# A graph-transformer network on one core: fp32 recurrent products, the last layer's projections among its graph attention, and norms measured tile by tile

## The chip, the cores and the metric

One Trainium2 chip, one of its cores. The whole network is one program. The metric is the device time of one execution in microseconds (us), the median of three. TensorE (PE) multiplies, VectorE (DVE) and ScalarE (ACT) do elementwise work, GpSimd (POOL) and SyncE (SP) mostly move data.

## The reference

625 nodes, 512 features, four layers on one residual array `X`, each with a graph part, a token mixer and a feed-forward part. Cut to what matters here:

```
L0: three SAGE convolutions (agg@Wl + h@Wr, layer norm, PReLU), linear attention, two small mixtures of experts
L1: two SAGE convolutions, slice attention; then an LSTM over the 625 nodes in order:
    for t in range(625):
        i, f, o, c~ = x[t] @ Wx + h @ Wh + b        # h: 512 values, Wh: 512 x 2048
        c = sigmoid(f) * c + sigmoid(i) * tanh(c~);  h = sigmoid(o) * tanh(c)
L2: linear attention, graph attention with an edge bias (found by sorting the edges), mixture of experts
L3: MLP 512-256-512, then graph attention (GAT):
        alpha[s, d] = exp(leaky_relu(a_src[s] + a_dst[d], 0.2) - max over the edges into d)
    and beside it linear attention on the same normalized X, then a layer norm; gated experts (8 of them)
```

A layer norm without scale, (x - mean) / sqrt(var + eps), stands before each half layer.

## The kernel before

`X` lies as five tiles of 125 rows by 512 columns. Products are in fp32 except those on one-hot and count data and those of the recurrence. Every product goes into one of four PSUM slots in turn (`TILES` gives their order and the engine that empties each); PE waits for a slot's last user. Weights come through a ring of four buffers of 1 MB in the order of `WEIGHTS`, loaded by SP: the load for a buffer waits until the last product of the weight four places earlier has been issued and done. Each engine runs its own program in order; semaphores tie them. `st.after()` on DVE waits for all that DVE itself has counted.

The recurrence (the loop over t). `h` is cut into four chunks of 128 (a column each). Its weights are cut for four strips of TensorE: strip q takes 128 of the 512 columns of each gate and writes PSUM partitions from 32q. The two halves f of the hidden units are worked in turn, so that the elementwise work of one lies beside the other's. In fp32 accuracy this is had from bf16: `Wh` was split before the loop into three bf16 parts (`L1f.split`, DVE, in the ring buffers), and `h` is split every step into three bf16 columns (`hidden_high`, `hidden_mid`, `hidden_low`, the last releasing PE by `ls_h`). `half(f, chunks)` (L929) then issues, for each chunk, part and strip, a product of 3 stationary columns with 256 moving ones: 96 a step. The order of a step:

```
PE:  wait h0; half 0 chunks 0,1; half 1 chunk 0; wait h1; half 0 chunks 2,3 -> full0; half 1 chunks 1,2,3 -> full1
DVE: turn0 (L1796), gather0 (L1801), product0, cell0, turn1, high0 (L1818), gather1, mid0, low0 (L1829), product1, cell1, high1, mid1, low1
ACT: tanh of the gates (L1258), tanh of the cell (L1262) for either half, the next step's x part, `keep` (h to ls_out)
```

`turn` is a 32x32 stream transpose that spreads the strips' results over 128 partitions; `gather` sums them with the x part. In 320 of the 625 steps a step of the edge sort stands between: two bf16 products of PE (L951), one DVE pass, in every second such step two ACT passes.

Norms (`normalize`): five `bn_stats` (L1432), five `bn_aggr` (L1435), a Newton inverse root in 15 small instructions with four rounds (L1414 to L1437), then one pass for each tile (L1447 in `norm_x`). `conv` follows it with scale, shift and PReLU, each as a pass over all five tiles.

The last layer: after `L3.adjT` PE spreads the attention's scalars (`L3.sdB`, L1103), DVE forms ten blocks `pT` of 125x625 in three passes (L2076, L2079, L2083), ACT takes exp, DVE multiplies by the counts (L2086), PE applies them (`L3.gat`), turns the result (`L3.gT`) and multiplies by W3 (`L3.gout`); then come q, k and v of linear attention (`qkv("L3")`), with POOL (`mins`), ACT (`exps`) and DVE (`feature_maps`) for their feature maps, then `attention("L3")`.

## Time and profile before

| | |
|---|---|
| median of three runs | 4932.3 us (4931.12 to 4932.89) |
| the profiled execution's own time | 4929.59 us |
| its span, first to last instruction | 4927.6 us |
| busy in it: PE, DVE, ACT, POOL | 3898.6, 2478.6, 1414.7, 345.7 us |
| mean granted TensorE clock | 0.962 of full speed |

### The profile page before, as it was taken

The page shows a single profiled execution, that of the slowest core. Times are in us where ns is not written, and L with a number is a line of the kernel's source. Part 1 is how long each engine was busy: PE and PEld are TensorE (multiplying, and loading weights), DVE is VectorE, ACT ScalarE, POOL GpSimd, SP SyncE. Part 2 cuts the span into 40 slices and gives each one's busy share as a digit, 9 for nine tenths or more (in the row PEclk, how much of TensorE's full clock was granted, in tenths as well). Part 3 has the DMA queues.
Part 4 walks back from the last instruction along what each step waited for, and adds up shares of the span by engine and source line. Part 5 has one row for each costly group of instructions (what it writes and reads, how often), then busy time and mean ns, then how long its engine had stood idle before and what let it go on. Part 6 is the DMA issues. An engine that isn't in the chain of part 4 may idle for free.

```text
span 4927.6 us, 161288 instructions
## 1 busy us (share of the span) xinstructions
PE 3898.6 (79%) x68148; PEld 2504.9 (51%) x68148; DVE 2478.6 (50%) x10718; ACT 1414.7 (29%) x4675; POOL 345.7 (7%) x314
## 2 busy tenths in 40 slices
PE   9878896877777666777777666666679996789998
PEld 7444453555555444555555444444446744545554
DVE  6323216477767555667776556665542535221111
ACT  0010111344444222444444222245531401011111
POOL 0000000000000222000000221012210000100000
PEclk9888998999999999999999999999999998889999
DMA  2000101200000000000000000000003301011111
GB/s 68 26 30 27 41 26 69 103 27 0 0 0 0 1 1 4 1 0 0 0 0 0 1 2 4 0 1 1 1 24 84 73 30 58 34 37 60 60 60 36
DMA packets 46351, 122.19 MB, mean 25 GB/s; under 512 B 24956, under 2 KB 32915, under 8 KB 35657
## 3 DMA queue, kind: packets, MB, share of 16 engines
q1 hardware_dynamic: 36490, 99.00, 5.9%
q0 software_dynamic: 9776, 22.00, 2.3%
q8 instruction: 60, 0.98, 0.1%
q14 instruction: 25, 0.20, 0.0%
HBM read 105.79 MB, written 14.92 MB: 24 GB/s over the span
## 4 chain that ended last, share of the span: by engine, by line
PE 62%; DVE 28%; issue 5%; ACT 4%; POOL 0%; DVEq 0%; ACTq 0%; POOLq 0%
PE PS L655 31%; PE PS L929 25%; DVE ls_turn L1796 11%; DVE ls_act L1801 4%; ACT ls_gate L1258 3%; PE PS L741 2%; DVE ls_pr L1805 2%; DVE ls_parts L1829 2%; DVE ls_parts L1824 1%; DVE ls_parts L1818 1%; PE PS L1026 1%; PE PS L686 1%; PE PS L1076 1%; DVE stats L1432 1%; PE PS L1016 1%
## 5 line engine op out<-in xcount | busy, mean ns | idle before, releaser
L929 PE MATMUL PS<-BUF,ls_parts 128*3 128x256 bf16 x60000 | 1856.8, 273 | 743.6 <-DVE ls_parts L1829 720.1
L929 PEld LDWEIGHTS PS<-BUF,ls_parts 128*3 128x3 bf16 x60000 | 1318.7, 84 | 1279.7 <-DVE ls_parts L1829 1107.1
L1796 DVE STREAM_TRANSPOSE ls_turn<-PS 128x256 f32<-128x256 f32 x1250 | 557.3, 446 | 488.5 <-PE PS L929 466.2
L655 PE MATMUL PS<-ring,BUF 128*125 128x512 f32 (+1 forms) x1440 | 617.8, 588 | 27.6 <-DVE BUF L1569 11.2
L655 PE MATMUL PS<-BUF,ring 128*128 128x512 f32 (+1 forms) x2176 | 594.6, 435 | 2.3 <-ACT BUF L1166 1.4
L1258 ACT ACTIVATE ls_gate<-ls_act 128x8 f32<-128x8 f32 x1250 | 261.6, 209 | 973.8 <-DVE ls_act L1801 970.5
L655 PEld LDWEIGHTS PS<-BUF,ring 128*128 128x128 f32 x2176 | 330.7, 191 | 273.1 <-issue 271.2
L655 PEld LDWEIGHTS PS<-ring,BUF 128*125 128x125 f32 x1440 | 270.5, 190 | 356.8 <-issue 333.2
L1262 ACT ACTIVATE ls_th<-ls_gate 128x2 f32<-128x2 f32 x1250 | 253.8, 203 | 454.9 <-DVE ls_gate L1810 454.9
L1174 ACT ACTIVATE BUF<-PS,cols 128x625 f32<-128x625 f32 x146 | 114.0, 782 | 712.8 <-PE PS L655 709.9
L1805 DVE SCALAR_TENSOR_TENSOR ls_pr<-ls_gate 128x4 f32<-128x4 f32 x1250 | 203.1, 162 | 178.1 <-ACT ls_gate L1258 173.5
L1818 DVE SCALAR_TENSOR_TENSOR ls_parts<-ls_gate,ls_th 128x2 f32<-128x2 f32 x1250 | 194.0, 155 | 149.9 <-ACT ls_th L1262 132.5
L1801 DVE TENSOR_REDUCE ls_act<-ls_turn 128x8 f32<-128x32 f32 x1250 | 232.3, 186 | 21.5
L1166 ACT ACTIVATE BUF<-PS 128x500 f32<-128x500 f32 (+1 forms) x100 | 50.4, 563 | 634.3 <-PE PS L686 633.9
L1829 DVE TENSOR_TENSOR ls_parts<-ls_parts 128x2 f32<-128x2 f32 x1250 | 205.1, 164 | 42.8
L1810 DVE SCALAR_TENSOR_TENSOR ls_gate<-ls_pr 128x2 f32<-128x2 f32 x1250 | 200.3, 160 | 43.0
L1824 DVE TENSOR_TENSOR ls_parts<-ls_parts 128x2 f32<-128x2 f32 x1250 | 197.6, 158 | 21.4
L1266 ACT ACTIVATE BUF<-ls_parts 128x4 f32 x625 | 132.0, 211 | 200.8 <-DVE ls_parts L1818 200.8
L605 POOL DMA_INDIRECT edges_by_cell<-duo x80 | 94.1, 1177 | 993.0 <-DVE ls_turn L1796 993.0
L605 POOL DMA_INDIRECT edges_by_dst<-duo x80 | 94.3, 1178 | 950.6 <-issue 700.9
L951 PE MATMUL PS<-AH,rows 125*125 125x512 bf16 (+1 forms) x640 | 153.5, 322 | 0.1
L2154 DVE TENSOR_TENSOR BUF<-BUF 128x2500 f32<-128x2500 f32 x8 | 22.1, 2763 | 258.7 <-ACT BUF L1174 258.7
(291 smaller groups left out, 3038.3 us busy)
## 6 DMA issues: line engine op xcount, KB each, us to landing
cell_bias<-BUF SPq DMA_DIRECT2D x5, 2441.4 KB
BUF<-cell_bias POOLq DMA_DIRECT2D x5, 2441.4 KB, 14.9
ring<-in_L_wo SPq DMA_DIRECT2D x11, 1024.0 KB, 4.8
ring<-in_L_wi SPq DMA_DIRECT2D x8, 1024.0 KB, 4.8
ring<-in_L_wg SPq DMA_DIRECT2D x8, 1024.0 KB, 4.8
ring<-in_L_wout SPq DMA_DIRECT2D x8, 1024.0 KB, 4.8
ring<-in_L_w SPq DMA_DIRECT2D x4, 1024.0 KB, 4.8
ring<-in_L_gnn_Wl SPq DMA_DIRECT2D x3, 1024.0 KB, 7.0
```

Source lines behind the costliest of these rows:

```text
L605: pool.indirect_dma_start(to, bass.IndirectOffsetOnAxis(ap=at[0:EP, i:i + 1], axis=0), row[0:EP, i, :], None).then_inc(scattered[k][u], 16)
L655: ins = nc.tensor.matmul(out, a, b, start=(j == 0), stop=(j == len(terms) - 1))
L929: ins = nc.tensor.matmul(ls_sum[f][32 * q:32 * q + 3, :].rearrange("p (j n) -> p j n", j=4), ls_cut[:, c, 1:6:2], ls_half[:, s, q, c, :, f ...
L1258: nc.scalar.activation(ls_gate[:, f, 0:8], ls_act[:, f, :], ACT.Tanh).then_inc(ls_sig[f], 1)
L1262: nc.scalar.activation(ls_th[:, f, :], ls_gate[:, f, 8:10], ACT.Tanh, scale=0.5).then_inc(ls_tanh[f], 1)
L1796: V.transpose(ls_turn[:, 8 * f:8 * f + 8, 1:33], ls_sum[f].rearrange("p (g n) -> p g n", g=8)).then_inc(ls_turned[f], 1)
L1801: V.reduce_sum(ls_act[:, f, :], ls_turn[:, 8 * f:8 * f + 8, 0:4], AX_X).then_inc(ls_pre[f], 1)
L1805: V.scalar_tensor_tensor(ls_pr[:, f, :], ls_gate[:, f, 0:4], 1.0, ls_gate[:, f, 6:10], ALU.add, ALU.mult).then_inc(ls_prod[f], 1)
L1810: V.scalar_tensor_tensor(ls_gate[:, f, 8:10], ls_pr[:, f, 2:4], 0.5, ls_pr[:, f, 0:2], ALU.mult, ALU.add).then_inc(ls_cell[f], 1)
L1818: V.scalar_tensor_tensor(ls_parts[:, k, 0], ls_gate[:, f, 4:6], 1.0, ls_th[:, f, :], ALU.add, ALU.mult).then_inc(ls_high[f], 1)
L1824: V.tensor_tensor(ls_parts[:, k, 1], ls_parts[:, k, 0], ls_cut[:, k, 1], ALU.subtract).then_inc(ls_mid[f], 1)
L1829: V.tensor_tensor(ls_parts[:, k, 2], ls_parts[:, k, 1], ls_cut[:, k, 3], ALU.subtract).then_inc(ls_h[f], 1)
```

## The change

1. The recurrence multiplies in fp32. `h` is one fp32 column a chunk (`ls_hid`), written by a single DVE instruction for each half; `hidden_mid` and `hidden_low` go, and so do `L1f.split` and its loads. Each chunk and strip is one fp32 product of 1 stationary and 256 moving columns, 32 a step. `gather` adds two columns instead of reducing four. `Wh` comes laid out by the host and is loaded by SP straight into its place (4 MB, after `L1.out`), then scaled in two DVE instructions. The `Wx` weights move up four places in the ring.
2. In the last layer q stands before `L3.sdB`, k before `L3.mxB`, v before `L3.gat`; the maps of q and k run among the graph attention. The blocks are formed as max(0.2 x - m, x - m): the first term by ACT with a bias (`L3.low`), the second and the max by one DVE pass, so each block has one DVE pass before exp instead of three.
3. `measure` takes a tile's statistics right after the instruction that finishes the tile, in all places; three Newton rounds instead of four; in `conv` and after `L3.out` the passes after the norm run tile by tile, scale and shift fused with the norm (four passes instead of five).

```diff
@@ half() on TensorE
-                            for s in range(3):
-                                for q in range(4):
-                                    ins = nc.tensor.matmul(ls_sum[f][32 * q:32 * q + 3, :].rearrange("p (j n) -> p j n", j=4),
-                                                           ls_cut[:, c, 1:6:2], ls_half[:, s, q, c, :, f, :],
-                                                           start=(c == 0 and s == 0), stop=(c == KC - 1 and s == 2))
+                            for q in range(4):
+                                ins = nc.tensor.matmul(ls_sum[f][32 * q:32 * q + 1, :].rearrange("p (j n) -> p j n", j=4),
+                                                       ls_hid[:, c:c + 1], ls_half[:, q, c, :, f, :],
+                                                       start=(c == 0), stop=(c == KC - 1))
@@ a step on VectorE
-                    V.reduce_sum(ls_act[:, f, :], ls_turn[:, 8 * f:8 * f + 8, 0:4], AX_X).then_inc(ls_pre[f], 1)
+                    V.tensor_tensor(ls_act[:, f, :], ls_turn[:, 8 * f:8 * f + 8, 0], ls_turn[:, 8 * f:8 * f + 8, 1],
+                                    ALU.add).then_inc(ls_pre[f], 1)
-                    hidden_high(0, t)
+                    hidden(0, t)
                     gather(1, t)
-                    hidden_mid(0, t)
-                    hidden_low(0, t)
                     product(1, t)
                     cell(1, t)
                     if between:
                         between()
-                    hidden_high(1, t)
-                    hidden_mid(1, t)
-                    hidden_low(1, t)
+                    hidden(1, t)
@@ SyncE; VectorE before the loop
+                    if name == "L2_wq":
+                        sp.wait_ge(*full("L1.out", NT - 1))
+                        for q in range(4):
+                            sp.dma_start(ls_w[:, q, :, :], io["L1_wh"][:, q, :, :]).then_inc(wh_in, 16)
+                dve.wait_ge(wh_in, 64)
+                make(V.tensor_scalar(wh4[:, :, 0:384], wh4[:, :, 0:384], 0.25, None, ALU.mult), "L1f.scaled")
+                make(V.tensor_scalar(wh4[:, :, 384:512], wh4[:, :, 384:512], 0.5, None, ALU.mult), "L1f.scaled")
@@ the statistics
+            def measure(src, t):
+                st.done(V.bn_stats(stats[0:R, t, :], src[:, t, :]))
+                st.after()
+                st.done(V.bn_aggr(mv[0:R, t, :], stats[0:R, t, :]))
-                for k in range(4):
+                for k in range(3):
@@ conv
+                    u = u5[:, t, :]
+                    st.done(V.scalar_tensor_tensor(u, u, m, row(f"L0_gnn_g{i}"), ALU.subtract, ALU.mult))
+                    st.after()
+                    st.done(V.scalar_tensor_tensor(u, u, r, row(f"L0_gnn_b{i}"), ALU.mult, ALU.add))
+                    st.after()
+                    st.done(V.tensor_scalar(hR[:, t, :], u, 0.0, slope, ALU.min, ALU.mult))
+                    st.after()
+                    ins = V.scalar_tensor_tensor(hR[:, t, :], u, 0.0, hR[:, t, :], ALU.max, ALU.add)
@@ the last layer on TensorE
+                pe.wait_ge(*weight_ready("L3_wq"))
+                dense_cols("L3.q", xnT, weight("L3_wq"), KC)
                 pe.wait_ge(*made("L3.sd"))
                 for j in range(4):
                     spread("L3.sdB", j, lambda t: sd[0:R, j, t:t + 1])
+                pe.wait_ge(*weight_ready("L3_wk"))
+                dense_rows("L3.k", [(xnT, weight("L3_wk"))])
                 pe.wait_ge(*made("L3.mx"))
                 for j in range(2):
                     spread("L3.mxB", j, lambda t: mxc[0:R, j, t:t + 1])
+                pe.wait_ge(*weight_ready("L3_wv"))
+                dense_rows("L3.v", [(xnT, weight("L3_wv"))])
@@ the last layer on VectorE
+                biased_rows("L3.k", kR, "L3_mix_bk", 0, NT)
+                map_q("L3")
+                st.after()
+                dve.wait_ge(*evacd("L3.mxB"))
                 for h in range(2):
+                    make(V.scalar_tensor_tensor(sB[:, h, :], sB[:, 2 + h, :], 0.2, mB[:, h, :], ALU.mult, ALU.subtract),
+                         "L3.less")
+                    st.done(V.tensor_tensor(sB[:, 2 + h, :], sB[:, 2 + h, :], mB[:, h, :], ALU.subtract))
+                st.after()
                 for j in range(10):
+                    dve.wait_ge(*made("L3.low", j + 1))
+                    make(V.scalar_tensor_tensor(pT[j], sB[:, 2 + j // 5, :], sd[0:R, j // 5, j % 5:j % 5 + 1], pT[j],
+                                                ALU.add, ALU.max), "L3.sub")
+                biased_rows("L3.v", vR, "L3_mix_bv", 0, 2)
                 for j in range(10):
                     dve.wait_ge(*made("L3.pexp", j + 1))
+                    make(V.scalar_tensor_tensor(pT[j], pT[j], 3.0e38, AC[0:R, j % 5, :], ALU.min, ALU.mult), "L3.pt")
+                biased_rows("L3.v", vR, "L3_mix_bv", 2, NT)
@@ ... L3.gat and L3.og as before, then
-                feature_maps("L3")
+                map_k("L3")
+                add_out("L3.gout", row("L3_gnn_b3"), None, False)
                 attention("L3", ALU.max, 1e-6)
@@ after L3.out
+                    st.done(V.scalar_tensor_tensor(u, u, m, row("L3_mix_gamma"), ALU.subtract, ALU.mult))
+                    st.after()
+                    make(V.scalar_tensor_tensor(Xr[:, t, :], u, r, Xr[:, t, :], ALU.mult, ALU.add), "L3.done")
```

## Rows read from the trace of the kernel before

**Rows 1.** The page: shares of the chain that ended last, by line.

```profile
PE PS L655 31%; PE PS L929 25%; DVE ls_turn L1796 11%; DVE ls_act L1801 4%; ACT ls_gate L1258 3%; PE PS L741 2%; DVE ls_pr L1805 2%; DVE ls_parts L1829 2%; DVE ls_parts L1824 1%; DVE ls_parts L1818 1%; PE PS L1026 1%; PE PS L686 1%; PE PS L1076 1%; DVE stats L1432 1%; PE PS L1016 1%
```

**Rows 2.** Windows: stretch, busy us by engine, granted clock, DMA share.

```profile
900.00:3636.00 2736.00, 1989.32 (x60648) 1380.77 (x60648) 1781.40 (x9269) 1086.14 (x4158) 283.32 (x242) 1.00 0.03 6
```

**Rows 3.** Timeline of one step: start, length, engine, line.

```profile
2701.07 0.44 DVE L1796 STREAM_TRANSPOSE ls_turn<-PS 128x256 f32<-128x256 f32 x1
...
2701.44 0.15 DVE L1818 SCALAR_TENSOR_TENSOR ls_parts<-ls_gate,ls_th 128x2 f32<-128x2 f32 x1
...
2701.84 0.16 DVE L1829 TENSOR_TENSOR ls_parts<-ls_parts 128x2 f32<-128x2 f32 x1
...
2702.06 0.86 PEld L929 LDWEIGHTS PS<-BUF,ls_parts 128*3 128x3 bf16 x36 [1.64 <-DVE ls_parts L1829]
...
2702.64 0.16 DVE L1818 SCALAR_TENSOR_TENSOR ls_parts<-ls_gate,ls_th 128x2 f32<-128x2 f32 x1 [0.27 <-ACT ls_th L1262]
...
2703.25 1.51 PEld L929 LDWEIGHTS PS<-BUF,ls_parts 128*3 128x3 bf16 x60 [0.33 <-DVE ls_parts L1829]
2704.20 0.45 DVE L1796 STREAM_TRANSPOSE ls_turn<-PS 128x256 f32<-128x256 f32 x1 [1.00 <-PE PS L929]
...
2705.42 0.44 DVE L1796 STREAM_TRANSPOSE ls_turn<-PS 128x256 f32<-128x256 f32 x1
```

**Rows 4.** Timeline, the fp32 products of two row strips.

```profile
3802.36 1.33 PE L1006 MATMUL PS<-BUF 64*125 64x512 f32 x8
```

**Rows 5.** Timeline, a stretch of full-width fp32 passes.

```profile
4198.26 34.51 PE L655 MATMUL PS<-ring,BUF 128*125 128x512 f32 x80
```

**Rows 6.** Timeline, a step with edge sorting.

```profile
2404.99 0.48 PE L951 MATMUL PS<-AH,rows 125*125 125x512 bf16 x2
```

**Rows 7.** Timeline, ahead of the recurrence, TensorE.

```profile
801.61 1.27 PE L908 MATMUL PS<-ident,small 125*125 125x125 f32 x10
809.35 10.77 PE L655 MATMUL PS<-AH,ring 128*128 128x512 f32 x32 [6.48 <-issue]
837.59 62.26 PE L655 MATMUL PS<-AH,ring 128*128 128x512 f32 x224 [17.46 <-DVE duo L1761]
```

**Rows 8.** Timeline, one norm between PE-bound stages.

```profile
580.92 3.06 DVE L1432 BATCH_NORM_STATS2 stats<-X 125x6 f32<-125x512 f32 x5
...
587.50 2.38 DVE L1447 TENSOR_SCALAR BUF<-X,mv,nw 125x512 f32<-125x512 f32 x5
```

**Rows 9.** Timeline, second convolution: last tile to attention.

```profile
337.08 0.69 DVE L1503 TENSOR_TENSOR BUF<-PS,rows 125x512 f32<-125x512 f32 x1 [6.17 <-PE PS L655]
...
361.31 0.14 DVE L1546 COPY ksd<-PS 64x1 f32<-64x1 f32 x1
```

**Rows 10.** Timeline, third convolution to the next norm.

```profile
438.22 0.69 DVE L1503 TENSOR_TENSOR BUF<-PS,rows 125x512 f32<-125x512 f32 x1 [6.17 <-PE PS L655]
...
474.30 3.06 DVE L1432 BATCH_NORM_STATS2 stats<-X 125x6 f32<-125x512 f32 x5
```

**Rows 11.** Timeline, last layer's graph attention and what follows.

```profile
4115.24 5.51 PE L1103 MATMUL PS<-ident,sd 125*125 125x125 f32 x40
...
4142.15 7.20 ACT L1382 ACTIVATE BUF<-BUF 125x625 f32<-125x625 f32 x10 [7.40 <-DVE BUF L2083]
...
4155.84 14.10 PE L655 MATMUL PS<-BUF 125*125 125x129 f32 x100 [21.82 <-DVE BUF L2086]
...
4172.31 7.96 PE L655 MATMUL PS<-ring,BUF 128*125 128x512 f32 x18 [0.52 <-issue]
...
4245.20 2.50 PE L655 MATMUL PS<-BUF 125*128 125x128 f32 x10 [12.43 <-DVE BUF L1497]
```

**Rows 12.** Windows: context products of linear attention, L2's, then L3's.

```profile
3756.00:3767.00 11.00, 9.67 (x82) 9.10 (x81) 3.03 (x17) 0.00 (x0) 0.00 (x0) 0.94 0.28 97
4245.00:4263.00 18.00, 17.23 (x80) 17.14 (x80) 1.82 (x13) 0.00 (x0) 0.00 (x0) 0.50 0.00 0
```

**Rows 13.** Timeline, the last norms.

```profile
4327.10 4.40 PE L686 MATMUL PS<-ident,BUF 125*128 125x125 f32 x20 [27.15 <-DVE BUF L1447]
```

More of the change, by code:

```diff
@@ L209, in network @@
     halves = {t[0]: t[3] for t in TILES}
-    weights = [w for w in WEIGHTS if (4 if w[3].startswith("split") else halves[w[3]]) <= last]
+    weights = [w for w in WEIGHTS if halves[w[3]] <= last]
     weight_at = {w[0]: n for n, w in enumerate(weights)}
@@ L293, in network @@
         ls_tanh = [sem(f"ls_tanh{f}") for f in range(2)]
-        ls_high = [sem(f"ls_high{f}") for f in range(2)]
-        ls_mid = [sem(f"ls_mid{f}") for f in range(2)]
+        wh_in = sem("wh_in")
         ls_h = [sem(f"ls_h{f}") for f in range(2)]
@@ L513, in _ @@
                         old = weights[n - RING][3]
-                        if old.startswith("split"):
-                            sp.wait_ge(*made("L1f.split", int(old[5:]) + 1))
-                        else:
-                            sp.wait_ge(*full(old, first[old][1] - 1))
+                        sp.wait_ge(*full(old, first[old][1] - 1))
                     sp.dma_start(ring[:, n % RING, 0:k * w].rearrange("p (k w) -> p k w", k=k),
@@ L916, in _ @@
                 pe.wait_ge(*evacd("L1f.gx3"))
-                pe.wait_ge(*made("L1f.split"))
+                pe.wait_ge(*made("L1f.scaled"))
                 pe.wait_ge(*made("sort.offs", 1))
@@ L1377, in copy_spread @@
                                                   ACT.Copy), stage, j)
+                act.wait_ge(*made("L3.sd"))
+                copy_cols("L3.q", lambda c: qT[:, c, :], KC, ACT.Identity, bias=lambda c: col("L3_mix_bq", c))
                 copy_spread("L3.sdB", 4, lambda j: sB[:, j, :])
+                exp_q("L3")
                 copy_spread("L3.mxB", 2, lambda j: mB[:, j, :])
                 for j in range(10):
+                    act.wait_ge(*made("L3.less", j // 5 + 1))
+                    make(nc.scalar.activation(pT[j], sB[:, j // 5, :], ACT.Identity,
+                                              bias=sdl[0:R, j // 5, j % 5:j % 5 + 1]), "L3.low")
+                for j in range(10):
                     act.wait_ge(*made("L3.sub", j + 1))
-                    make(nc.scalar.activation(pT[:, j, :], pT[:, j, :], ACT.Exp), "L3.pexp")
+                    make(nc.scalar.activation(pT[j], pT[j], ACT.Exp), "L3.pexp")
+                exp_k("L3")
                 copy_turned("L3.gT", colsof(B(3), 2), 2)
-                copy_cols("L3.q", lambda c: qT[:, c, :], KC, ACT.Identity, bias=lambda c: col("L3_mix_bq", c))
-                exps("L3")
                 copy_turned("L3.oT", oT)
@@ L1484, in _ @@
             dve.wait_ge(x_in, 16)
+            for t in range(NT):
+                measure(Xr, t)
             norm_x("L0")
@@ L1969, in _ @@
                 attention("L2", ALU.add, 1e-6)
-                add_out("L2.out", row("L2_mix_b_proj"), None)
+                add_out("L2.out", row("L2_mix_b_proj"), None, False)
                 def biased(i):
@@ L2015, in _ @@
                 dve.wait_ge(*made("L2f.prob"))
-                add_out("L2f.s2", row("L2_ffn_sb2"), None)
+                add_out("L2f.s2", row("L2_ffn_sb2"), None, False)
                 for j in range(2):
@@ L2098, in _ @@
                     make(V.tensor_tensor(og[:, t, :], og[:, t, :], row("L3_gnn_bias_g", 256), ALU.add), "L3.og")
-                add_out("L3.gout", row("L3_gnn_b3"), None)
-                for stage, dst, bias in (("L3.k", kR, "L3_mix_bk"), ("L3.v", vR, "L3_mix_bv")):
-                    for t in range(NT):
-                        dve.wait_ge(*full(stage, t))
-                        took(V.tensor_tensor(dst[:, t, :], bank(stage, t)[0:R, :], row(bias), ALU.add), stage, t)
-                feature_maps("L3")
+                map_k("L3")
+                add_out("L3.gout", row("L3_gnn_b3"), None, False)
                 attention("L3", ALU.max, 1e-6)
+                for t in range(NT):
+                    st.done(V.tensor_tensor(Xr[:, t, :], Xr[:, t, :], row("L3_mix_beta"), ALU.add))
                 for t in range(NT):
@@ L2209 @@
     halves = {t[0]: t[3] for t in TILES}
-    used = [x[0] for x in WEIGHTS if (4 if x[3].startswith("split") else halves[x[3]]) <= LAST]
+    used = [x[0] for x in WEIGHTS if halves[x[3]] <= LAST]
     arrays = {name: chunked(w[name]) for name in used}
+    arrays["L1_wh"] = np.ascontiguousarray(
+        np.stack([a["L1_ffn_W_" + x][512:].reshape(4, 128, 4, 4, 32) for x in "ifoc"]).transpose(2, 4, 1, 0, 3, 5)
+    ).reshape(128, 4, 4, 512)
     arrays["x"] = a["x"]
```

172 lines of the change are left out of this document (67 added, 105 removed), and 9 rows, old and new, of tables (TILES, WEIGHTS).

## The prediction

> **What bounds the kernel now.** First the page's chain: what ended last was PE for most of it, at the fp32 products' line L655 (31%) and the recurrence's L929 (25%), with the DVE and ACT lines of the recurrence between [rows 1]. The windows then say how long the recurrence is: 2736 us of the 4928, PE at the full 2.4 GHz and busy 73% of it [rows 2]. Since 625 equal steps make it up, one step's timeline is the next view: 4.35 us from one turn1 to the next [rows 3]. In it the reader sees that turn1 (2701.07) comes right before high0, low0 releases PE at 2702.06 (block A, 36 products), low1 releases block B (60 products) at 2703.25, and turn0 starts 0.95 us into B. Between A and B PE stands still, for h1. So a step is a loop through PE's block A and B, turn0 and the elementwise work. The rest (2190 us) is mostly PE-bound fp32 work, with holes: 17.46 and 6.48 us ahead of the recurrence [rows 7], 21.82 and 12.43 us in the last layer [rows 11], 27.15 us at the last norms [rows 13], some 8 us at each norm.
>
> **The step in fp32: PE.** Before, 24 weight loads more take 1.51 - 0.86 = 0.65 us [rows 3]: four strips work at once, a wave of four products each 0.108 us, 24 waves a step, 2.6 us. After: 32 products of two passes each, 64 passes. A pass of 512 columns takes 34.51/80 = 0.431 us [rows 5], so one of 256 takes 0.216. If four strips again run at once there are 16 waves of 0.216: 3.45 us. That is 0.86 us more PE work a step, not less. Whether they do is the large unknown: no fp32 product on column strips stands in this trace. The nearest row is fp32 on two row strips: four products, eight passes (four of 512 columns, four of 113) within 1.33 us [rows 4]; one after another they would stream 4 x (0.431 + 0.095) = 2.10 us, two at once 1.05 us plus the fill. So two fp32 streams do overlap fully, though each product's two passes follow one another in the program. I take four at once; the ends are 16 waves (none lost) and 64 passes one by one (13.8 us a step).
>
> The Trainium skill, "TensorE: Matmul & The Clock Gate", Part 3 (Packing small matmuls), says that matmuls start and end strictly in program order and only weight loads are pulled ahead. By it the second pass of strip 0 would hold back strip 1's first; what that makes is the third rival below. The eight passes in 1.33 us don't agree with it, unless the two passes are not issued next to each other.
>
> **The step in fp32: the loop.** DVE loses mid and low of both halves. Four of its 160 ns instructions go, and on the h1 side 0.4 us of wait (high1 2702.64 to PE 2703.25 is 0.61, of which one instruction and its signal, 0.22 as from low0 to PE, stay). Gather gets some 0.03 shorter. But PE's longer blocks take it back. Two loops, from the same rows. (a) Through turn0: turn0 to turn1 1.22 - 0.03 = 1.19 (2704.20 to 2705.42); turn1 to high0 0.37; high0 to PE 0.22; A is 6 waves, then B's first 4 waves, so 9 waves to the start of the last = 1.94; from there to turn0 0.51 (before: 0.95 less 5 waves of 0.108 is 0.41, and the stream is 0.107 longer). Sum 4.23. (b) Through turn1: it needs full1, all 16 waves: 0.37 + 0.22 + 15 x 0.216 + 0.51 = 4.34. h1 is there before A ends: turn1 to high1 is 1.57, less 0.03, plus 0.22 = 1.76 after turn1, A ends at 0.59 + 1.29 = 1.88. So PE no longer waits for h1; it has become the bound of the step, held only by h0, which DVE makes after turn1. Loop (b) is the longer: 4.34 against 4.35. **The recurrence gains 625 x 0.01 = 6 us: nothing worth naming.** PE streams for 3.45 us of a step instead of 2.6. Bounds if four strips overlap: 4.23 if turn1 doesn't wait (-73 us), 4.42 if a wave costs 2.5% more (+45 us).
>
> The sort steps: PE's two extra products take 0.48 us [rows 6]; B now ends about 1.0 us after turn0 and block A starts 1.88 after it, so they still fit, and the 0.9 us DVE pass moves to where mid1 and low1 were. Nothing.
>
> **Ahead of the recurrence.** PE got the first Wx only with the ring's fourth turn (6.48 idle before 809.35) and then stood 17.46 us for DVE, which evacuates `sort.ind` only after the split [rows 7]. Both holes go: Wx is loaded during L1, DVE has no split, and its two scalings (8192 elements a partition, at most the price of the old four on the same data) lie under 70 us of PE work. Wh's 4 MB are issued at the end of L1.out, on SP's queue ahead of L2_wq only, which waits for a Wx buffer anyway; they have those same 90 us. PE then runs its 256 passes at 62.26/224 = 0.278: 71.2 us, from 802.9 (end of the row at 801.61) less the 3.2 us of the norm before it: 870.9. Before: 837.59 + 62.26 = 899.85. **-29 us** (the norm's 3.2 within). Bounds -24 (a wait for Wh or a cold PE start) and -29.
>
> **Norms.** One in front of PE: from the last tile to the first normalized one 587.50 - 580.92 = 6.58 us: 3.06 and 0.49 for the statistics, 15 small instructions of 0.20 [rows 8]. After: one tile's statistics behind the last tile, about 0.95, and 12 small ones, 2.4: 3.35. **-3.2 each**, where tiles come slower than DVE takes them: before L1, L1f (counted above) and L2f: -6.4. Where DVE itself sets the pace the statistics come one by one with their waits, about 0.9 a tile instead of 0.7: L0 +0.3, L2 (after the five `L1f.hs`) +0.7, L3 (after L2f's experts) -0.4: +0.6.
> conv1 holds back attention: 337.08 to 361.31, 24.2 us [rows 9]. After: bias, add, statistics of the last tile 2.4, Newton 2.6, five tiles of four dependent passes (three 0.69, one 0.54, each + 0.04) 13.7: 18.7. **-5.5.** conv2 with `L0.out`: 438.22 to 474.30 plus a norm of 6.6, 42.7 us [rows 10]; after 2.4 + 2.6 + 17.2 + five tiles of 2.3 + 2.4 = 36.1: **-6.1** (the rest is rounding). conv0 lies under q, k, v: 0.
> Last norms: PE stands 27.15 us before 4327.10 [rows 13]: two norms of 6.6 with 2.4, 3.1, 3.1, 3.1 between. After: 0.95 + 2.4 + five tiles of 1.4 + five statistics of 0.9 + 2.4 = 17.3, against 25.0: **-7.5.**
>
> **The last layer.** Before: sdB at 4115.24, PE idle 21.82 before `L3.gat` at 4155.84, gout at 4172.31, q k v 51.7 us (1.5 x 34.51), 12.43 idle for the maps, attention at 4245.20 [rows 5, 11]. After, each instruction in its queue: q 4115.2 to 4132.6; sdB to 4138.1 (its 17 us delay is new: DVE has nothing else); DVE's max pass 7.4, so mx at 4146.8; PE k to 4155.4, mxB to 4158.2; DVE k's bias, map of q (exp done by ACT meanwhile, after sdB's copies) to 4159.2, the four row passes to 4162.2; ACT's ten `low` 4160.0 to 4167.3; DVE's ten blocks to 4169.6; ACT's exps (ten take 7.20 [rows 11]) to 4174.5; DVE two v tiles, then ten products (7.3) to 4178.4. PE's v ends at 4175.3, so PE idles 3 us where it idled 21.8. gat, gT from 4178.4 in 14.3 (16.5 less the cold first tile), gout 8.7: attention at 4201.4, DVE's map of k done by 4195, POOL's minima (five of 1.46 behind map of q) by 4167. 4245.2 - 4201.4 = 43.8. And PE comes to attention warm: its 80 passes were busy 17.23 us at the low clock (0.50, 1.2 GHz) after the 12.43 us idle, the same work in L2 9.67 at 0.94 [rows 12]: 8 more, and 1 in what follows. **-53 us.** Bounds: -35 (one more chain link of DVE or ACT late) and -60.
>
> **Sum.** -6 - 29 - 6.4 + 0.6 - 5.5 - 6.1 - 7.5 - 53 = -113 us. Against the profiled execution, 4929.6 (span 4927.6): 4817. The median of the runs is 2.7 higher: 4819 us.
>
> **Rivals.**
> (1) DVE gets to h0 by loop (a): 4.23 a step, -73 in the recurrence: 4752 us. For it: the last products' tail may overlap turn1's start. Against: the arithmetic of (b) has no slack but that. 0.14.
> (2) The last layer's chain, now with two 17 us stages in front of its DVE work, comes late: half of the 53 lost, 4846 us. For it: sdB and mxB are queued behind q and k, and everything of DVE and ACT hangs on them. Against: PE then has work in all of that time. 0.16.
> (3) Slower: the fp32 streams on four column strips hold each other back. In program order with each product's second pass first: 33 slots of 0.216 instead of 16 waves, a step of 0.59 + 32 x 0.216 + 0.51 = 8.0 us, (8.0 - 4.35) x 625 - 107 = +2174: 7106 us. Since PE is the bound, little is enough: all else gains 107 us, 0.17 a step, so it decides from a wave of 0.228, 5.5% above 0.216. At a quarter more (0.27) a step is 5.20 and the time 5356 us. For it: four streams of 4-byte data from all partitions are in no row. Against: [rows 4]. 0.16, 0.07 for the full price.
> (4) The step is as forecast, but holes close by less, or a wave is 3 to 5% dearer: within 10 us of before, 4932. 0.03.
> The forecast: 0.51.
>
> **Numbers.** 0.2% of the time, 10 us, is what a measurement tells from no change. Faster: 0.51 + 0.14 + 0.16 = 0.81; same 0.03; slower 0.16. The range goes from rival (1) to the forecast with waves 4% dearer and (2): 4745 to 4905; above it lies rival (3).
>
> **What would show it.** In the step's timeline: waves of four passes at 0.216 us, 64 matmul records a step; no idle of PE between A and B, full1 setting turn1; a period of 4.3 us; mid and low gone. Ahead of the recurrence: no wait for `duo`, first recurrent product near 872. In the last layer: a PE idle of a few us before gat, q, k, v before it, attention at the full clock. Wrong would be a wave beyond 0.228, a PE idle of over 10 us before gat, or a step far from 4.34.

## The result and the profile after

The kernel after takes 4775.41 us (median; 4773.79 to 4776.27 in 4 runs) against 4931.93 of before in the same session: ratio 0.9681, interval 0.9667 to 0.9696. Forecast were 4819 us, so the gain is 156 us where 113 were expected. The profiled execution of after took 4776.09 us, its span is 4774.4. Cut at the same events, the two spans differ as follows (us).

```
stretch                                      before    after     difference  forecast
start to the first turn0                     904.12    865.99    -38.1       -43.5
first to last turn0 (624 steps)             2729.6    2670.7     -58.9        -6
last turn0 to L3.adjT                        472.1     469.9      -2.2        -2.9
L3.adjT to the last output tile              194.2     150.3     -43.9       -52 (the 53 less 1)
last norms                                    26.4      18.7      -7.7        -7.5
experts to the end                           601.2     598.9      -2.3        -1
```

The profiled executions differ by 153.5 us, the medians by 156.5. So the recurrence gave 53 us more than forecast, and all else 13 us less. The row from the last turn0 to `L3.adjT` is the least certain: it contains layer L2, and from the norm before L2 to the norm before L2f the traces of one and the same code (all those below that have the new norms) take from 279.6 us (after) to 289.8 (rec_norms), the longer ones with more time at the low clock. The page of after, the chain that ended last by line [rows 1]:

```profile
PE PS L654 30%; PE PS L927 29%; DVE ls_turn L1803 6%; ACT ls_gate L1268 3%; DVE ls_pr L1813 2%; DVE ls_act L1808 2%; PE PS L740 2%; DVE ls_gate L1818 2%; DVE ls_hid L1825 2%; PE PS L1024 1%; PE PS L685 1%; ACT ls_th L1272 1%; ACT AH L1290 1%; ACT AH L1293 1%; PE PS L1074 1%
```

The recurrence in a window (stretch, its length, busy us of PE, PE's weight loads, DVE, ACT and POOL, granted clock, DMA share, GB/s) [rows 2]:

```profile
870.00:3530.00 2660.00, 2394.06 (x40418) 1010.54 (x40414) 1422.05 (x6735) 1078.61 (x4134) 283.34 (x241) 1.00 0.03 5
```

PE is busy 90% of it instead of 73%, at the same full clock, and yet it is shorter. One step of after, timeline [rows 3]:

```profile
2701.43 3.63 PE L927 MATMUL PS<-BUF,ls_hid 128*1 128x256 f32 x64 [0.62 <-DVE ls_hid L1825]
...
2702.44 0.16 DVE L1825 SCALAR_TENSOR_TENSOR ls_hid<-ls_gate,ls_th 128x2 f32<-128x2 f32 x1 [0.27 <-ACT ls_th L1272]
...
2703.91 0.45 DVE L1803 STREAM_TRANSPOSE ls_turn<-PS 128x256 f32<-128x256 f32 x1 [1.31 <-PE PS L927]
...
2705.14 0.45 DVE L1803 STREAM_TRANSPOSE ls_turn<-PS 128x256 f32<-128x256 f32 x1
...
2705.51 0.12 DVE L1825 SCALAR_TENSOR_TENSOR ls_hid<-ls_gate,ls_th 128x2 f32<-128x2 f32 x1
...
2705.69 0.39 PE L927 MATMUL PS<-BUF,ls_hid 128*1 128x256 f32 x3 [0.62 <-DVE ls_hid L1825]
```

All 64 passes are one stretch of 3.63 us: h1 (2702.44) is written before block A ends (2702.73), and nothing stops PE between blocks A and B. In the single records the passes start in waves of four, 0.216 us apart, the four within 20 ns. The period is 4.254 us (2701.43 to 2705.69 here), before 4.347. Ahead of the recurrence, TensorE [rows 7]:

```profile
790.73 1.26 PE L907 MATMUL PS<-ident,small 125*125 125x125 f32 x10
791.83 69.39 PE L654 MATMUL PS<-AH,ring 128*128 128x512 f32 x256
...
863.51 2.77 PE L927 MATMUL PS<-BUF,ls_hid 128*1 128x256 f32 x48
```

Both holes of before are gone; the 256 passes are one row. A norm between PE-bound stages, the timeline of DVE [rows 8]: from the last statistics (573.05) to the first normalized tile 3.43 us, and one tile's 0.72 ahead of it, 4.15 from the last tile where it was 7.30.

```profile
573.05 0.69 DVE L1447 BATCH_NORM_STATS2 stats<-X 125x6 f32<-125x512 f32 x1
...
576.48 2.37 DVE L1464 TENSOR_SCALAR BUF<-X,mv,nw 125x512 f32<-125x512 f32 x5
```

The last layer, timeline of TensorE [rows 11], and the last norms [rows 13]:

```profile
4034.62 4.54 PE L1101 MATMUL PS<-ident,sd 125*125 125x125 f32 x40
4039.00 17.33 PE L654 MATMUL PS<-ring,BUF 128*125 128x512 f32 x40
4056.16 2.35 PE L1101 MATMUL PS<-ident,mxc 125*125 125x125 f32 x20
4058.35 13.90 PE L654 MATMUL PS<-ring,BUF 128*125 128x512 f32 x32
4073.28 3.70 PE L654 MATMUL PS<-ring,BUF 128*125 128x512 f32 x8 [1.04 <-DVE BUF L2075]
4081.08 2.52 PE L654 MATMUL PS<-BUF 125*125 125x129 f32 x10 [4.10 <-DVE AH L2092]
...
4097.56 8.82 PE L654 MATMUL PS<-ring,BUF 128*125 128x512 f32 x20 [0.52 <-issue]
4106.22 1.28 PE L654 MATMUL PS<-BUF 125*128 125x128 f32 x10
...
4176.19 3.71 PE L685 MATMUL PS<-ident,BUF 125*128 125x125 f32 x20 [19.41 <-DVE BUF L1464]
```

PE's idle of 21.82 ahead of `L3.gat` has become 1.04 and 4.10, and the 12.43 ahead of attention is gone. Windows of after (first L3.gat, then the context products) show that PE was still at the lower clock for parts of both (0.51 and 0.54; it was 0.50 in [rows 12]):

```profile
4083.00:4087.00 4.00, 4.00 (x21) 4.00 (x21) 1.12 (x4) 0.00 (x0) 0.00 (x0) 0.51 0.00 0
...
4110.00:4121.00 11.00, 9.60 (x50) 9.54 (x49) 2.34 (x16) 0.00 (x0) 0.00 (x0) 0.54 0.05 22
```

### The profile page after: what moved, and what is told of

Same layout as the page of the kernel before. It is cut to its first block, busy times and chain, and to the rows that moved or that the text cites. A ratio compares the mean times of both kernels' runs of the same rounds, so it can differ in the third digit from the quotient of the medians.

```text
span 4774.4 us, 118664 instructions
## 1 busy us (share of the span) xinstructions
PE 4313.0 (90%) x48148; PEld 2136.0 (45%) x48148; DVE 2083.9 (44%) x8065; ACT 1419.9 (30%) x4685; POOL 349.2 (7%) x314
## 4 chain that ended last, share of the span: by engine, by line
PE 66%; DVE 19%; issue 8%; ACT 6%; DVEq 0%; POOL 0%; ACTq 0%; POOLq 0%
PE PS L654 30%; PE PS L927 29%; DVE ls_turn L1803 6%; ACT ls_gate L1268 3%; DVE ls_pr L1813 2%; DVE ls_act L1808 2%; PE PS L740 2%; DVE ls_gate L1818 2%; DVE ls_hid L1825 2%; PE PS L1024 1%; PE PS L685 1%; ACT ls_th L1272 1%; ACT AH L1290 1%; ACT AH L1293 1%; PE PS L1074 1%
## 5 line engine op out<-in xcount | busy, mean ns | idle before, releaser
L927 PE MATMUL PS<-BUF,ls_hid 128*1 128x256 f32 x40000 | 2275.8, 379 | 266.8 <-DVE ls_hid L1825 266.8
L927 PEld LDWEIGHTS PS<-BUF,ls_hid 128*1 128x1 f32 x40000 | 954.7, 83 | 1516.9 <-DVE ls_hid L1825 672.6
L1825 DVE SCALAR_TENSOR_TENSOR ls_hid<-ls_gate,ls_th 128x2 f32<-128x2 f32 x1250 | 178.2, 143 | 150.2 <-ACT ls_th L1272 133.7
L1808 DVE TENSOR_TENSOR ls_act<-ls_turn 128x8 f32<-128x8 f32 x1250 | 216.2, 173 | 21.5
L1276 ACT ACTIVATE BUF<-ls_hid 128x4 f32 x625 | 130.7, 209 | 200.1 <-DVE ls_hid L1825 200.1
L949 PE MATMUL PS<-AH,rows 125*125 125x512 bf16 (+1 forms) x640 | 153.5, 322 | 0.0
L685 PE MATMUL PS<-ident,BUF 125*128 125x125 f32 x390 | 62.1, 326 | 95.0 <-DVE BUF L1464 79.8
L1263 ACT ACTIVATE ls_turn<-BUF 128x16 f32 (+1 forms) x625 | 135.6, 217 | 0.0
```

The costliest lines, as they stand in the source:

```text
L927: ins = nc.tensor.matmul(ls_sum[f][32 * q:32 * q + 1, :].rearrange("p (j n) -> p j n", j=4), ls_hid[:, c:c + 1], ls_half[:, q, c, :, f, :] ...
L949: ins = nc.tensor.matmul(PS[0:EP, 1, a:b], m, hot_rank[u][:, a:b], start=False, stop=False, skip_group_check=True)
L1263: nc.scalar.activation(ls_turn[:, :, 0], ls_gx[:, :, bass.ds(t, 1)].rearrange("p g o -> p (g o)"), ACT.Copy).then_inc(ls_gxin, 1)
L1808: V.tensor_tensor(ls_act[:, f, :], ls_turn[:, 8 * f:8 * f + 8, 0], ls_turn[:, 8 * f:8 * f + 8, 1], ALU.add).then_inc(ls_pre[f], 1)
L1825: V.scalar_tensor_tensor(ls_hid[:, 2 * f:2 * f + 2], ls_gate[:, f, 4:6], 1.0, ls_th[:, f, :], ALU.add, ALU.mult).then_inc(ls_h[f], 1)
```

## The experiments

Ratios are against the kernel before, run beside them.

**1. rec_only and rec_norms: the parts of the change one after the other.** rec_only is the kernel before with the recurrence's part of the diff alone:

```
-  for s in range(3): for q in range(4): matmul(ls_sum[f][32*q:32*q+3], ls_cut[:, c, 1:6:2], ls_half[:, s, q, c, :, f, :])
+  for q in range(4): matmul(ls_sum[f][32*q:32*q+1], ls_hid[:, c:c+1], ls_half[:, q, c, :, f, :])
-  the split of Wh;  hidden_mid, hidden_low     +  L1_wh loaded behind L1.out, two scalings
```

> The kernel before with the recurrence and its loads alone changed (fp32 products, Wh loaded at the end of L1, no split); norms and last layer as before. Theory 1, from the two traces: a step is 4.254 us instead of 4.347, and the gain of the recurrence does not depend on the other edits, so 625 x 0.093 = 58, and 26 to 30 us ahead of it: 4932 - 86 = 4846 us (4838 to 4852), step 4.254. Rival, the forecast's sum: -6 and -26, so 4900 us, and the rest of the measured gain of 156 us sits in norms and last layer.

Measured: 4849.36 us (4841.14 to 4850.27; ratio 0.9834, 0.9818 to 0.985), as Theory 1 had it; step 4.250, first turn0 at 873.99 instead of 904.12. rec_norms adds `measure` per tile, the three-round Newton and the fused passes, and lacks only the last layer's order.

> The same with the norms changed too; only the last layer's order is that of before. Theory 1 (parts read off the two traces: conv1 -5.9, conv2 with L0.out -5.6, the norms before L1 and L2f -3.2 each, last norms -7.7, L2 and L3 +2.2, and some 4 to 6 us given back where PE comes to a stage earlier and at a lower granted clock): 4846 - 20 = 4826 us (4818 to 4832), and the kernel after is then 44 to 50 us faster by its last layer. Rival: the norms gain their full 27 us here and the last layer only 40: 4819 us.

Measured: 4821.4 us (4819.49 to 4831.64; 0.9775, 0.9759 to 0.9792). So the three parts give 82, 28 and 46 us, each with some us of spread between executions, and the recurrence's gain of 0.097 a step is there without the other edits: the forecast's 4900 us for this part is out. The two expectations for rec_norms lie too close together for the times to tell. The traces do: its first turn0 comes at 863.42, only 10.6 us ahead of rec_only, while conv1 (-5.9), conv2 with `L0.out` (-5.6) and two norms (-3.2 and -3.3) make 18.0 when each is measured between its own ends. The rest is given back in the stages between. rec_only and rec_norms differ in the norms alone, and the windows show at which clock the stage runs that ends with L1's norm, first rec_only, then rec_norms:

```profile
478.00:584.60 106.60, 91.27 (x320) 52.13 (x320) 35.37 (x101) 14.42 (x29) 0.72 (x2) 0.88 0.13 47
```

```profile
466.60:573.90 107.30, 95.07 (x320) 54.92 (x320) 35.87 (x99) 14.46 (x29) 2.80 (x6) 0.85 0.12 40
```

The 320 passes are busy 3.8 us longer, and the stage takes 107.3 us instead of 106.6, though its norm is 3.2 shorter. Behind L1's norm the same is seen at 0.97 instead of 0.98: from that norm to L1f's it is 203.1 us for 204.0, where 3.3 were saved. This isn't chance: the four traces with the old norms have 106.6 or 106.7 at 0.88, the ten with the new ones 107.2 to 107.4 at 0.85. So the shorter norms lead to it; which change of PE's idle times sets off which fall of the clock is not shown.

**2. high_only and two_parts: what the removed instructions are worth.** On the kernel before.

```
high_only:  ls_cut[:, c, 1:6:2] -> ls_cut[:, c, 1:2]      (M = 1; hidden_mid, hidden_low gone)
two_parts:  ls_cut[:, c, 1:6:2] -> ls_cut[:, c, 1:4:2]    (M = 2; hidden_low gone)
            for s in range(3)   -> for s in range(2)
```

> The kernel before, with h's middle and low part left out of the recurrence (its output is less exact): PE has the same 96 bf16 products a step, DVE four instructions fewer, and PE waits for high0 and high1. It splits the change of a step in two. Theory 1 (two loops, with the offsets of the trace after): h1 sets it: turn0 to h1 2.78, release 0.18, five waves of 0.108 for half 0's last two chunks, 0.41 to turn0: 3.91 us a step; so leaving out mid and low is worth 0.44 and fp32's longer streams take 0.34 of it back. 4932 - 625 x 0.44 = 4658 us. Rival: PE's blocks set the step of before as they do after; then it stays near 4.25 and the time near 4870.

Measured: 4713.27 us (0.9557, 0.9538 to 0.9577), 55 us above the expected 4658; step 3.96 in the median, mean 4.02. One step of it, timeline:

```profile
2701.81 3.18 PE L929 MATMUL PS<-BUF,ls_parts 128*1 128x256 bf16 x96 [0.91 <-DVE ls_parts L1818]
...
2703.02 0.74 PEld L929 LDWEIGHTS PS<-BUF,ls_parts 128*1 128x1 bf16 x29 [0.35 <-DVE ls_parts L1818]
...
2704.24 0.45 DVE L1796 STREAM_TRANSPOSE ls_turn<-PS 128x256 f32<-128x256 f32 x1 [1.27 <-PE PS L929]
```

Block B waits for h1 (2703.02), and turn0 comes 1.22 behind that. So the change of a step is two large terms of opposite sign: without mid and low the bf16 step falls from 4.347 to 3.96 (-0.39), and fp32 gives back 0.30 by its longer streams. 0.1 is left. The expected 3.91 was 0.05 low, and the mean is another 0.06 above the median, in the steps with sorting (4.02) as in those without (4.03).

> The kernel before, with the low part of Wh and the low part of h left out (64 bf16 products a step on two rows; its output is less exact). Theory 1: mid stays in the chain of h1 (0.16, and 0.04 to 0.06 more by mid0 ahead of gather1), four products fewer a chunk: turn0 to PE's block B 3.16, three waves of 0.108, 0.41: about 3.9 to 3.95 us a step, 4932 - 625 x 0.42 = 4670 us. Rival: DVE's instructions and not their waits set the step, so that it comes out at 4.1 or more (4780 us).

Measured: 4744.0 us (0.962, 0.9601 to 0.9639), 74 us above the expected 4670 and 31 us slower than high_only. The median step is 3.935 in the steps with sorting, as expected, and 3.97 in those without; the mean is 4.07. The windows name what the median hides, the granted clock (a stretch with sort products, then one without):

```profile
1275.00:1400.00 125.00, 78.89 (x2062) 47.47 (x2066) 83.68 (x421) 58.09 (x218) 0.00 (x0) 1.00 0.00 0
1650.00:1775.00 125.00, 80.54 (x1960) 47.15 (x1960) 68.67 (x364) 35.00 (x182) 35.29 (x30) 0.81 0.03 2
```

The 0.81 is a mean: PE goes back and forth between its two levels, 1.2 and 2.4 GHz (1.00 in the window from 1648 to 1658, 0.52 in that from 1658 to 1668).

**3. half1_short: which loop binds after.**

```
-  half(1, (1, 2, 3)).then_inc(ls_full[1], 1)
+  half(1, (2, 3)).then_inc(ls_full[1], 1)
```

> The kernel after with one of half 1's four chunks of h left out of the recurrent product (two waves of block B less; its output is another). It shortens only the loop through full1 and turn1, by 2 x 0.216, and leaves the loop through turn0 as it is. Theory A (both loops close at 4.254, turn0's binds as soon as the other is shorter): the step stays at 4.24 to 4.25 and the time within 10 us of 4775. Theory B (the forecast: the loop through turn1 is the longer by 0.1): the step falls to about 4.15, 4712 us. Theory C (PE's work alone sets the step): it falls by 0.43, 4505 us.

Measured: 4775.67 us (0.9685, 0.9665 to 0.9704), step 4.253. Two waves less, 0.43 us of PE work a step, change nothing: the loop through turn0 (a) sets 4.25 by itself, as Theory A had it. PE, busy 90% in after, isn't the bound. turn1 comes 1.206 us behind turn0 here and 1.224 in after, so in after it does wait 0.02 for `full1`; PE's release, 0.200 here and 0.178 there, makes up for it.

**4. q_outer and pairs: how column strips share PE.** The order of a block's products in the kernel after.

```
q_outer:  for c in chunks: for q in range(4):   ->  for q in range(4): for c in chunks:
pairs:    for pair in (chunks[:2], chunks[2:]): for q in range(4): for c in pair:
```

> The kernel after with the order of the products in a block turned: all chunks of column strip 0, then those of strip 1, and so on; same products, same values. Theory A (each strip takes its products from a short look-ahead, and strips overlap only where neighbouring products go to different strips): block A's half 0 has two products, four passes, on a strip before the next strip begins, so little overlaps and a step is 7 us or more: over 6400 us. Theory B (strips run on their own, as far as the program runs ahead): waves of four as before, step 4.25 to 4.4.

Measured: 5551.35 us (1.1258, 1.1235 to 1.128), step 5.505: neither theory. Windows over the q_outer step, 0.43 us (two waves) each; x counts the passes that touch the stretch, and the last figures are clock and DMA:

```profile
1502.64:1503.07 0.43, 0.43 (x5) 0.18 (x5) 1.00 0.00 0
1503.07:1503.50 0.43, 0.43 (x8) 0.18 (x6) 1.00 0.00 0
1503.50:1503.93 0.43, 0.43 (x9) 0.18 (x6) 1.00 0.00 0
1503.93:1504.36 0.43, 0.43 (x7) 0.17 (x3) 1.00 0.00 0
```

PE is busy in all of it, but with two or three strips. The records don't name the strip; it is read off the chains of passes 0.216 us apart. Block A, two products a strip, starts all four strips within 44 ns (the 31 ns of the next expectation is the distance to the third). Half 1's part of block B has three a strip: strip 0 starts at 1502.235, strip 1 at 1502.672 (with strip 0's second product), strip 2 at 1503.108, strip 3 at 1503.538. From that came a model: products are issued in program order; a strip holds one running and one waiting; a third for the same strip holds back all behind it.

> The kernel after with at most two chunks in a row on a strip: within a pair of chunks strip 0's two products, then strip 1's, and so on. In q_outer the block with two products a strip started all four strips within 31 ns, and the block with three a strip started strip 1 only with strip 0's second product, strip 2 another product later, strip 3 another. Theory A (products are issued in program order, and a strip takes one running and one waiting product; a third holds back all that follow): never more than one waits here, so waves of four as before: step 4.25 to 4.27, 4775 to 4790 us. Theory B (the look-ahead counts products and not strips, some three or four of them): with pairs strip 2 and 3 start late, a step of 4.6 or more, 5000 us.

Measured: 4805.03 us (0.9748, 0.9728 to 0.9767), step 4.300, against 4.6 or more by a look-ahead that counts products. Each of four stretches of two waves shows 14 passes, the first of them here:

```profile
1502.78:1503.21 0.43, 0.43 (x14) 0.19 (x5) 1.00 0.00 0
```

The model holds, though the time is 15 us above the range given. The 0.046 more a step is not explained in full: the four of a wave start within 45 ns and not 20, which would make 0.025 of it. The Trainium skill, "TensorE: Matmul & The Clock Gate", Part 3, says that matmuls start and end strictly in program order. On four column strips they don't start in that order here, if the strips are read rightly: in q_outer strip 1's first product (fourth in the program) started at 1502.672, strip 0's third at 1503.098.

**5. kmin_late: the last layer's missing 7 us.** On the kernel after, in `mins`:

```
-  pool.wait_ge(*made("L3.qfm"))
+  pool.wait_ge(*made("L3.pt"))
```

> The kernel after with POOL's five minima of k in the last layer started behind the ten mask products and not behind q's map, so that POOL no longer works beside DVE's row passes and ten blocks. In the trace after POOL's five take 9.70 us instead of 7.30, two row passes of DVE 1.22 and 1.21 instead of 0.7, the ten blocks 9.03 instead of 7.4. Theory 1 (POOL and DVE slow each other down): they go back to 0.7 to 0.8 each, the L3.gat products start 1 to 2 us earlier against L3.adjT, and the whole is 0 to 2 us faster (4774). Rival: ACT's chain of low and exp sets it; then the DVE passes get shorter and L3.gat comes at the same time.

Measured: 4769.43 us (0.9675, 0.9656 to 0.9695; 4766.38 and 4772.49). POOL's row, after and here:

```profile
L551 POOL TENSOR_SCALAR BUF<-BUF 125x512 f32<-125x512 f32 x5 | 9.7, 1963 | 22.6 <-DVE BUF L1513 22.6
```

```profile
L554 POOL TENSOR_SCALAR BUF<-BUF 125x512 f32<-125x512 f32 x5 | 7.3, 1487 | 41.8 <-DVE AH L2095 41.8
```

and the timeline here:

```profile
4057.60 0.80 DVE L2086 TENSOR_TENSOR BUF<-BUF 125x625 f32<-125x625 f32 x1
...
4059.88 3.99 DVE L2090 SCALAR_TENSOR_TENSOR BUF<-BUF,sd 125x625 f32<-125x625 f32 x5
4063.78 3.98 DVE L2090 SCALAR_TENSOR_TENSOR AH<-BUF,sd,AH 125x625 f32<-125x625 f32 x5
...
4076.21 1.68 PE L657 MATMUL PS<-BUF 125*125 125x129 f32 x10 [3.50 <-DVE AH L2095]
```

The row pass is back from 1.22 to 0.80, the ten blocks from 9.03 to 7.97, PE's idle of 1.04 is gone, and `L3.gat` starts 63.2 us after q instead of 65.1: Theory 1, and the rival falls. The size of the whole was not expected. The medians differ by 6 us, for 0 to 2, but the two ratios' intervals overlap; the traces tell more. From the norm before L3 to the one behind it all seven traces with the early minima and the new order take 203 us, this one 194.1 and best_five, which has the late minima too, 194.2. The experts then take 601.0 instead of 598.9 in both, so 6.8 us remain. Most of it comes behind gat: from q's start to the last numerator product 111.5 us instead of 120.3. PE idles 0.6 less at gat and has one idle fewer, comes through the first ten gat passes in 1.68 instead of 2.52, and from the start of attention to the first numerator product takes 18.2 us instead of 22.7, at a mean granted clock of 0.79 in attention's first 64 us instead of 0.75.

**6. best_two to best_five: a version that beats both.** Expected first:

> The kernel after, with the recurrent product in two bf16 parts of Wh and of h (64 products of 0.108-us streams a step instead of 64 passes of 0.216; less exact than fp32, more exact than one bf16 part), the split made by DVE under the Wx products, and mid0 taken behind gather1, where DVE waits for ACT anyway. From two_parts (median step 3.935, mean 4.07): step 3.88 to 3.90, mean 4.02, so 4775 - 624 x 0.26 = 4613 us (4600 to 4650). The split costs nothing, as DVE's 20 us of it lie under some 55 us of PE. Rival: the split is late and costs 10 us or more; or mid0 behind gather1 delays block A enough to hold block B: then 4650 or more.

> best_two with 24 products more a step, into a PSUM bank that nobody reads, in the idle time of PE behind block B (0.65 us of work a step). In two_parts the granted clock was 1.00 in the recurrence's first 600 us and then 0.80 to 0.85 for stretches of some 400 us, while PE was busy 63%; high_only, busy 80%, kept 1.00. Theory 1 (the clock goes by how busy PE is kept): the clock stays at 1.00 and the step's mean falls by 0.02 to 0.05, 10 to 30 us faster than best_two. Rival: the clock falls as before, or the extra products hold back block A; then as slow as best_two or slower.

```
best_two:   two bf16 parts of Wh (made in place of the fp32 copy) and of h; hidden_mid(0) behind gather(1)
best_heat:  for s in range(6): for q in range(4):
                matmul(PS[32 * q:32 * q + 2, 2, 0:256], ones, ls_half[q][:, 0, 0, :, 0, :])   # behind block B
```

Measured: best_two 4691.38 us (0.9511, 0.9495 to 0.9527), a miss by 78; best_heat 4644.5 (0.9419, 0.9403 to 0.9435). The split cost nothing (first turn0 at 864.75), and the steps without sorting came to 3.92 in the median. But the clock fell as in two_parts, and beyond that to 0.94 to 0.99 in the windows with sorting, and the sort steps took 4.11 in the mean, 4.01 in two_parts. The windows of best_two, then of best_heat:

```profile
1650.00:1775.00 125.00, 79.83 (x1984) 46.82 (x1980) 69.18 (x372) 35.82 (x186) 36.47 (x31) 0.82 0.03 1
```

```profile
1650.00:1775.00 125.00, 87.61 (x2816) 60.58 (x2816) 71.09 (x383) 36.83 (x192) 37.73 (x32) 1.00 0.04 2
```

24 products whose result nobody reads keep PE at 2.4 GHz and save 47 us, for the 10 to 30 expected. What remains is ACT, in best_heat's timeline of a sort step:

```profile
1305.54 0.82 ACT L1299 ACTIVATE AH<-iota,AH 125x625 f32<-125x625 f32 x1
...
1306.39 0.82 ACT L1302 ACTIVATE AH<-AH,ones 125x625 bf16<-125x625 f32 x1
...
1306.57 0.18 DVE L1827 TENSOR_REDUCE ls_act<-ls_turn 128x8 f32<-128x24 f32 x1
1307.12 0.19 ACT L1277 ACTIVATE ls_gate<-ls_act 128x8 f32<-128x8 f32 x1
```

gates0 could start at 1306.77 and starts at 1307.12, behind the second 0.82. My copy of h had been moved to wait for mid1, which made both later.

```
    act: keep(t)          -  wait_ge(ls_h[1], t + 2)       +  wait_ge(ls_high[1], t + 1)
    act: rank_pass        -  step; step; rank_hot (Abs, Relu)
                          +  step; rank_far (Abs); step; rank_hot (Relu)
```

> best_heat with ACT's two sort operations of 0.82 us in two different steps and not in one, and the copy of h behind high1 instead of mid1. In the sort steps of best_heat every other step is 4.3 us or so, because gates0 waits for the second of them (mean 4.09 against 3.91 in steps without). Theory 1: the sort steps fall to 3.92 to 3.97, 320 x 0.14 = 45 us: 4600 us (4592 to 4612). Rival: the rank products on PE or DVE's rank pass hold the sort steps as well, and half of it or less comes: 4620 us or more.

Measured: 4567.04 us (0.9264, 0.9248 to 0.9279); sort steps 3.913. It is 33 better than expected: the sort steps stood at 4.09 and went all the way down, and the last 86 steps fell from 4.16 to 3.97 too. Those are the steps behind the exp of the sorted edges, and in each ACT loads a function table ahead of gates0, which takes 1.28 us. In best_heat:

```profile
3201.94 1.28 ACT L1277 ACT_TABLE_LOAD   x1
...
3202.77 0.18 DVE L1827 TENSOR_REDUCE ls_act<-ls_turn 128x8 f32<-128x24 f32 x1
...
3203.23 0.21 ACT L1277 ACTIVATE ls_gate<-ls_act 128x8 f32<-128x8 f32 x1
```

The load starts 0.1 behind the copy of h. That copy comes 0.2 earlier behind high1 in best_three, so gates0 starts 0.27 behind gather0's start there (3202.05, 3202.32) and not 0.46. In after the load is over before gather0 starts and costs nothing. How much of the gain in the sort steps is the copy's and how much the parting of Abs and Relu was not run apart.

```
best_five:  turn0 gather0 turn1 product0 gather1 cell0 hidden0 product1 mid0 cell1 hidden1 mid1
   so far:  turn0 gather0 product0 cell0 turn1 hidden0 gather1 mid0 product1 cell1 hidden1 mid1
```

> best_three with the late minima of kmin_late and another order on DVE in a step: turn1 right behind gather0, in the time in which DVE waits for ACT's gates0, and not behind cell0. In best_three a step is 3.912 and PE's block B is released by mid1, 3.18 after turn0; its last product of half 1 starts 0.24 after the next turn0, so full1 is there at about 0.65, just before gather0 ends (0.66). Theory 1: turn1 starts at 0.68 instead of 1.21, product0 0.12 later, h0 0.12 later; ACT's gates1 comes right behind tanh0, product1 at 1.91, mid1 gives block B free at about 2.97: a step of 3.70, in the sort steps 3.75 at most, so 4567 - 6 - 624 x 0.2 = 4436 us (4420 to 4470). Rival: full1 is late for the new order, turn1 then holds product0 and h0, and the step stays at 3.9 or grows: 4560 us or more.

Measured: 4274.91 us (0.8664, 0.865 to 0.8678), step 3.456: 161 us below the expected 4436. Of the 292 us to best_three the recurrence has 282 in the traces. One step of it, timeline:

```profile
2500.88 0.45 DVE L1832 STREAM_TRANSPOSE ls_turn<-PS 128x256 f32<-128x256 f32 x1 [0.79 <-PE PS L935]
...
2501.46 0.45 DVE L1832 STREAM_TRANSPOSE ls_turn<-PS 128x256 f32<-128x256 f32 x1
...
2502.56 0.17 DVE L1841 SCALAR_TENSOR_TENSOR ls_pr<-ls_gate 128x4 f32<-128x4 f32 x1
...
2503.39 0.16 DVE L1859 TENSOR_TENSOR ls_parts<-ls_parts 128x2 f32<-128x2 f32 x1
...
2503.60 0.97 PEld L935 LDWEIGHTS PS<-BUF,ls_parts 128*2 128x2 bf16 x40 [0.20 <-DVE ls_parts L1859]
2504.34 0.45 DVE L1832 STREAM_TRANSPOSE ls_turn<-PS 128x256 f32<-128x256 f32 x1 [0.79 <-PE PS L935]
```

turn1 starts 0.58 after turn0 (expected 0.68, before 1.21), product1 1.68 (expected 1.91), block B is released at 2.72 instead of the 2.97 expected: I had laid DVE's instructions end to end, but independent ones start some 0.1 us apart, and ACT's gates1 began 0.11 behind tanh0. The price of the time is exactness: Wh and h are carried by two bf16 parts, not in fp32. What the new order of DVE would give with fp32 products was not run.

## Why the forecast was right, and where it was off

**The recurrence: "Loop (b) is the longer: 4.34 against 4.35" was the step that failed, by the size of its terms.** The waves were as forecast (0.216, sixteen, four strips at once). Loop (b) measures 0.374 + 0.178 + 15 x 0.2158 + 0.467 = 4.256: the release of PE is 0.18 instead of 0.22, the last wave to turn1 0.47 instead of 0.51. Both had been read off the step of before, the release behind low0 and not behind high0 (0.20 in high_only), the 0.51 from turn0's gap and not from turn1's. Loop (a) measures 1.224 + 0.374 + 0.178 + 9 x 0.2158 + 0.536 = 4.254 instead of 4.23. They close together, and half1_short shows that (a) alone gives the same step. That (b) alone would was not run. Two terms 0.04 too long, times 625, are the missing 53 us: the gain was a difference of 0.1 between removed and added work of 0.3 to 0.4 each (experiment 2), and the forecast had no more digits than that. The time fell inside the range because the range began at rival (1), not because the step of the forecast was right: the recurrence came 53 us lower and all else 13 us higher than forecast. The statement that PE had become the bound is wrong too.

**The rivals.** (1), the step at loop (a), is what happened to the recurrence, at 4.254 and not 4.23. (3) didn't happen in the order chosen; q_outer shows strips held back in another order and by another rule (three products in a row to one strip), at 5.5 us a step. (4), a time near 4932, did not come. (2) is out: the last layer gave 46 (rec_norms to after).

**Ahead of the recurrence, -29:** from L1f's first normalized tile to the first turn0 rec_only takes 85.4 us where before takes 112.6. That is -27.2 without any norm, for 25.8 forecast (29 less the norm's 3.2). Wh was there, no wait for `duo`. The sign "first recurrent product near 872" left out what the stages ahead of this one gain; with the forecast's own -43.5 it would have been 859 (902.19 in before), and it came at 863.51.

**Norms:** conv1 -5.9 (-5.5), conv2 -5.6 (-6.1), before L1 and L2f -3.2 and -3.1 (-3.2), last norms -7.7 (-7.5). Three small ones: L0 -0.05 (+0.3), L2 +0.5 (+0.7), L3 -0.3 (-0.4), each from its first tile (L0: its first statistics) to the first normalized one. Each was priced right to 0.5 us between its own ends; that what it saves can be given back by a colder PE in the stages around it (experiment 1) was priced nowhere.

**The last layer, -53:** -46. Moved by the 99.2 us by which `L3.adjT` came earlier, each event up to `low` was within 1.2 us of its forecast (mx 4047.8 for 4047.6). Then the ten blocks took 9.0 for 7.4, since POOL's minima worked beside DVE: I had checked only that POOL would be ready. gat to gout took 16.5 as before, not 14.3: PE had idled 5 us and ran at 0.51 again, and of the 8 us for a warm attention 4.3 came (its 80 passes end 12.9 us behind its start and not 17.2).

## What to carry to other kernels

In a loop of small dependent instructions write every loop that closes with its terms in tenths of an instruction, from the row of the same instruction pair; a gain that is the difference of two large terms has the error of both. Then look for an independent instruction that can start while its engine waits for another engine (turn1 behind gather0): that exchange took 282 us off the recurrence between best_three and best_five, more than any other edit here. On TensorE's column strips, let neighbouring products go to different strips and never three in a row to one. And when PE gets less to do, read the granted clock in windows before you trust the median step; compare stages over several traces, since the same code differs by up to 10 us in one stage here.
